# ScalarE's order within a step of a fused deformable convolution, attention and routing kernel

## The chip, the cores and the metric

The kernel runs on one core of one Trainium2 chip. The metric is device time in microseconds (us). The core has five engines with instruction streams of their own: TensorE (PE in the profile, its weight loads PEld), VectorE (DVE), ScalarE (ACT), GpSimd (POOL) and SyncE (SP), which only issues DMAs. An engine takes its stream in order; what belongs to another engine is waited for with semaphores.

## The reference, cut to what matters

The input holds 8 images of 128 channels and 56 x 56 pixels, in float32. The first layer adds a deformable convolution of the normalised image. The second treats the 3136 pixels of an image as tokens, adds causal attention, and then adds a mixture of 64 experts in which each expert takes its 8 best tokens of an image.

```
offset = conv3x3(groupnorm(x), offset_w) + offset_b        # 18 offsets for each pixel
x_off  = sum of 4 weighted gathers of groupnorm(x) at pixel + tap + offset   # 9 taps
x      = x + conv3x3_stride3(x_off, conv_w)

t      = tokens(x)                                          # (8, 3136, 128)
scores = (ln(t) Wq^T)(ln(t) Wk^T)^T / sqrt(128), causal
t      = t + softmax(scores) (ln(t) Wv^T)

probs  = softmax over the tokens of (ln(t) gate_w^T + gate_b)   # 64 experts
vals, idx = top 8 tokens of each expert
pooled = sum over the 8 of vals * token
out_e  = gelu([pooled, 1] weight1) weight2 (with bias row)
t      = t + scatter-add of out_e * vals to the tokens idx
```

## The kernel before

An image is 25 tiles of 128 pixels; 8 images make 200 tiles. One loop of steps runs over them, one step for a tile, and each engine has the same loop in its own stream. A step is a pipeline slice. In step s of image b:

- the convolution works on tile s of image b. Its nine gathered blocks of 128 x 128 are held in one of five ring buffers. ScalarE multiplies the first cell of each gathered pair by a weight (`scale_first`, L620, nine instructions in three pieces), VectorE adds the second (`add_second`, L889). Both work two or three tiles ahead of the tile that TensorE convolves. TensorE turns the nine blocks (`turn_samples`, L1201), ScalarE copies them out of PSUM (`keep_samples`, L625, three copies), and TensorE multiplies them (`products`, L1209);
- the scores are those of the tile six steps back (TensorE L1227, VectorE L901 adds the mask and takes the maximum, L1019 ends the maximum);
- softmax and attention are those of the tile seven steps back. ScalarE takes the exponentials (L721), TensorE turns the row of probabilities in pieces of 512 columns (`turn_prob`, L1236), ScalarE copies each piece to SBUF (`keep_prob`, L639), and TensorE multiplies it with the values (`attend`, L1250). VectorE adds the result to the tokens in the next step (L934, counted by `t2_done`), and only then may the next tile's attention overwrite the one PSUM bank of attention.

A tile i of an image has i + 1 blocks of 128 keys, so its row has one piece in tiles 0 to 3, two in tiles 4 to 7, three in tiles 8 to 11, and so on. Since attention runs seven steps behind, **one-piece steps are steps 7 to 10 of an image, and two-piece steps are 11 to 14**.

Everything else is hung into the steps by a table written by hand (MISC, L79 on). An entry says at which step, in which place of the step (E, F, M or L, in this order), which work for which image is done. TensorE fills a PSUM bank in that place (`fill_misc`) and ScalarE or VectorE empties it in the same place of its own stream (`keep_misc`). Those of place M in the steps concerned are the offset convolutions of the next image (`chunk`, steps 5 to 11, 12 matrix products of TensorE at L1111 and L1116, copied out by ScalarE at L648), the routing probabilities (`pm`, step 12), a block of queries (step 13) and the pooled tokens (step 14, emptied by VectorE). Place L holds `turn_xf` (L1141, copied at L665), `keys` (L1128, copied at L652), `query` (L1136, copied at L662) and `pm`.

All PSUM work but attention's sums goes through seven banks in a fixed order (RING_ORDER): a bank's seventh next user waits until its content was taken away.

The routing of the image before runs in steps 9 to 13: VectorE replaces the best eight logits (L1054, step 9), ScalarE takes exponentials of 64 x 3136 logits in four instructions (L737, two in step 10 and two in step 11), VectorE keeps the chosen ones (L1058). The next image's sampling indices are computed by VectorE in steps 13 to 17 (L830 to L862, nine instructions of it in step 13).

GpSimd issues nine indirect gathers for each tile, in order, as far ahead as the ring of five lets it. The last part of the kernel, from about 2576 us on, runs the experts and writes the output.

Of the kernel before, what the change touches and what calls it, by code (L numbers as in the profile page):

```python
# [11 lines left out]
ACT = mybir.ActivationFunctionType  # L12
# [3 lines left out]
B, C, H, W = 8, 128, 56, 56  # L16
# [77 lines left out]
LREPLACE, LEXP, LCHOSEN = 9, (10, 10, 11, 11), (11, 11, 12, 12)  # L94
SHARES = [(k, min(2 * CHUNK, N - k)) for k in range(0, N, 2 * CHUNK)]
# [10 lines left out]
def misc_at(step, place):  # L106

    b, s = divmod(step, TILES)
    return [(what, b + d, n) for t, at, what, d, n in MISC if t == s and at == place and 0 <= b + d < B]
# [45 lines left out]
def width_of(t):  # L155

    return (HALF_KEYS + 1 if split(t) else t % TILES + 1) * P


def chunks_of(i):  # L160

    total = width_of(i)
    return [(k, min(CHUNK, total - k)) for k in range(0, total, CHUNK)]


def chunks_in(t):

    return len(chunks_of(t % TILES)) if 0 <= t < ALL else 0
# [7 lines left out]
def rows_of(step):  # L176

    b, s = divmod(step, TILES)
    n = s - ROWS_STEP
    return [(b + 1, n)] if b + 1 < B and 0 <= n < ROW_GROUPS else []  # L180


def ahead(step):

    b, s = divmod(step, TILES)
    if b == 0 and s < AHEAD_TWO:
        return 1
    if AHEAD_THREE <= s < BACK_TO_TWO:
        return 3
    return 2  # L190
# [62 lines left out]
def image_of(t):  # L253

    return divmod(t, TILES)
# [72 lines left out]
def first_part(nc, x_cm, x_tok, off_w, off_b, conv_w, wq, wk, wv, gate_w, gate_b, w1, w2, base, b1_t, b2, pooled, ident, shared, w_in,  # L328
               c_base, c_ident, c_mask, c_group, pair_table, t2_dram, pm_dram, rz_dram):
    with ExitStack() as ctx:  # L330
        def sb(name, shape, dt=F32):
            return ctx.enter_context(nc.sbuf_tensor(name, shape, dt))
# [4 lines left out]
        def sem(name):  # L337
            return ctx.enter_context(nc.semaphore(name))
# [47 lines left out]
        logit = sb("logit", [E, NP])  # L386
        lmax = sb("lmax", [E, 1])
        zsum = sb("zsum", [E, len(SHARES)])
# [45 lines left out]
        replaced, lexp_done, rz_done, chosen = sem("replaced"), sem("lexp_done"), sem("rz_done"), sem("chosen")  # L434
# [11 lines left out]
        def prob_at(t, k0, w):  # L446

            start = 0 if t % 2 == 0 else PROB_COLS - width_of(t)
            return prob[:, start + k0:start + k0 + w]
# [149 lines left out]
        def _(act):  # L599
            after = Waits(act)  # L600

            def normalise(k, part):

                after(affine_done, k + 1)
                y0, y1 = part * H // PARTS, (part + 1) * H // PARTS
                inner = xpad[:].rearrange("p (y x) -> p y x", x=XW)[:, 1 + y0:1 + y1, 1:1 + W]
                given = first_image.rearrange("p (y x) -> p y x", x=W)[:, y0:y1, :] if k == 0 else inner
                act.activation(inner, given, ACT.Identity, bias=nb[:, 0:1], scale=rs[:, 0:1]).then_inc(normalised, 1)
# [14 lines left out]
            def keep_samples(t, p):  # L623
                after(smp_tp, PIECES * t + p + 1)
                act.activation(smp_t[p][:], ring_bank(("smp", t, p))[:, 0:3 * P], ACT.Copy).then_inc(smp_ev, 1)  # L625

            def keep_rows(k, n):

                at = ROW_GROUPS * k + n
                after(rows_tp, at + 1)  # L630
                after(rows_stored[at % 2], 32 * (at // 2))
                act.activation(rows_out[at % 2][:], ring_bank(("rows", k, n))[:].rearrange("p (i c) -> p i c", c=C),
                               ACT.Copy).then_inc(rows_ev, 1)

            def keep_prob(t, c):
                w = chunks_of(t % TILES)[c][1]
                q = CHUNKS_BEFORE[t] + c
                after(prob_tp, q + 1)
                act.activation(prob_t[q % 3][:, 0:w], ring_bank(("prob", t, c))[:, 0:w], ACT.Copy)\  # L639
                   .then_inc(prob_ev, 1)  # L640
# [37 lines left out]
            for h in range(2):  # L678
                at = h * HALF_IMAGE
# [28 lines left out]
            for step in range(END):  # L708
                b, s = image_of(step)
                v = step - LAG_V  # L710
                samples_first = step < ALL and chunks_in(step - LAG_S) == 1
                if samples_first:
                    for p in range(PIECES):
                        keep_samples(step, p)
                if 0 <= v < ALL:

                    r = v % 2
                    after(max_done, v + 1)
                    after(t2_done, v - 1)
                    row = prob_at(v, 0, width_of(v))  # L720
                    act.activation(row, row, ACT.Exp, bias=nmax[r][:, 0:1], accum_out=total[r][:, 0:1])\  # L721
                       .then_inc(exp_done, 1)
                if step < ALL and not samples_first:
                    for p in range(PIECES):
                        keep_samples(step, p)
                for use in misc_at(step, "E"):
                    keep_misc(use)
                for k, n in rows_of(step):
                    keep_rows(k, n)
                for use in misc_at(step, "F"):  # L730
                    keep_misc(use)
                if 0 <= b - 1 < B:
                    for k, (at, w) in enumerate(SHARES):
                        if s == LEXP[k]:
                            after(replaced, b)
                            after(rz_done, b - 1)
                            act.activation(logit[:, at:at + w], logit[:, at:at + w], ACT.Exp, bias=lmax[:, 0:1],  # L737
                                           accum_out=zsum[:, k:k + 1]).then_inc(lexp_done, 1)
                if chunks_in(v):
                    keep_prob(v, 0)  # L740
                parts = list(range(PARTS)) if s == NORMALISE and b + 1 < B else []
                early = chunks_in(v) >= 3
                pieces = sample_pieces(step)
                while pieces and not early:
                    scale_first(*pieces.pop(0))
                if chunks_in(v) >= 2:
                    keep_prob(v, 1)
                for c in inner_rounds(step):
                    if c + 1 < chunks_in(v):
                        keep_prob(v, c + 1)  # L750
                    if c == 1:
                        for use in misc_at(step, "M"):
                            keep_misc(use)
                    if early and pieces:
                        scale_first(*pieces.pop(0))
                    if c >= 2 and parts:
                        normalise(b + 1, parts.pop(0))
                for t, p in pieces:
                    scale_first(t, p)
                for use in misc_at(step, "L"):  # L760
                    keep_misc(use)
                for part in parts:
                    normalise(b + 1, part)
# [304 lines left out]
        def _(pe):  # L1068
            after = Waits(pe)
# [121 lines left out]
            for step in range(END):  # L1191
                ts, v = step - LAG_S, step - LAG_V
                b, i = image_of(step)
# [20 lines left out]
                def scores(c):  # L1214
                    tb, ti = image_of(ts)
                    k0, w = chunks_of(ti)[c]
                    emptied(after, ("query", tb, ti // PER))
                    free_ring(("score", ts, c))
                    k, at = GPI * tb + ti // PER, ti % PER * P
                    bank = ring_bank(("score", ts, c))  # L1220
                    if split(ts):
                        for h in range(2):
                            first = k0 + h * HALF_KEYS * P if k0 < HALF_KEYS * P else (TILES - 1) * P
                            last = pe.matmul(bank[h * ROWS_HALF:(h + 1) * ROWS_HALF, 0:w], qt[k % 2][:, at:at + ROWS_HALF],
                                             key_chunk(tb, first, w), start=True, stop=True)
                    else:
                        last = pe.matmul(bank[:, 0:w], qt[k % 2][:, at:at + P], key_chunk(tb, k0, w), start=True, stop=True)  # L1227
                    last.then_inc(scored, 1)
# [52 lines left out]
                for c in rounds:  # L1281
                    if c + 1 < chunks_in(v):
                        turn_prob(c + 1)
                    if c + 2 < chunks_in(ts):
                        scores(c + 2)
                    if c - 1 < chunks_in(v):
                        attend(c - 1)
                    if c == 1:
                        for use in misc_at(step, "M"):
                            fill_misc(use)  # L1290
                if rounds.stop - 1 < chunks_in(v):
# [337 lines left out]
```

## Time and profile before

| what | value |
|---|---|
| median of 3 runs | 2722.27 us (2721.83 to 2726.87) |
| the profiled execution | 2730.18 us |
| its span, first to last instruction | 2728.2 us |
| TensorE busy (PE) | 2547.9 us, 93% |
| weight loads busy (PEld) | 2044.1 us, 75% |
| VectorE busy | 1888.0 us, 69% |
| ScalarE busy | 1778.7 us, 65% |
| GpSimd busy | 1773.3 us, 65% |
| mean granted TensorE clock | 0.973 |

A busy share is that of the whole span; the ends of matrix products are modelled, and consecutive products overlap a little in the rows, so a distance between two starts tells more than a duration. The line numbers are those of the kernel file. Idle time of an engine stands in brackets behind the instruction that ended it, with what released it.

### The profile page before, as it was taken

How to read it: one execution, taken by the hardware profiler on the slowest of the kernel's cores; microseconds unless marked ns; L12 is line 12 of the kernel's file. 1: busy time of each engine (PE TensorE's matmuls, PEld its weight loads, DVE VectorE, ACT ScalarE, POOL GpSimd, SP SyncE). 2: the span in 40 equal slices, each digit the busy share in tenths (PEclk: the TensorE clock that was granted, in tenths of full speed). 3: DMA queues.
4: the chain of work that ended last, by engine and by line, in shares of the span. 5: the costliest groups of instructions: out<-in, count | busy, mean ns of one | idle time of the engine just before them, and what ended most of it. 6: DMA issues, size and time to landing. Idle time of an engine off the chain costs nothing. (4 is left out here: it accounts for less than half of the span.)

```text
span 2728.2 us, 53901 instructions
## 1 busy us (share of the span) xinstructions
PE 2547.9 (93%) x19262; PEld 2044.1 (75%) x19262; DVE 1888.0 (69%) x7300; ACT 1778.7 (65%) x4144; POOL 1773.3 (65%) x1831
## 2 busy tenths in 40 slices
PE   4688999999999999999999999999999998999687
PEld 3466787788878887788877887788778887787564
DVE  4456776886678767876688776877688766775425
ACT  3455667776677767677776767776777667765320
POOL 4777776777667775777677776777677776750000
PEclk8799999999999999999999999999999999999789
DMA  6354333653356334643356334634355333432299
GB/s 189 112 159 134 118 112 117 159 139 113 103 158 152 117 114 119 158 132 113 94 172 149 114 108 130 164 118 121 100 168 148 113 111 110 119 85 97 83 392 394
DMA packets 218149, 382.63 MB, mean 140 GB/s; under 512 B 43785, under 2 KB 128713, under 8 KB 216987
## 3 DMA queue, kind: packets, MB, share of 16 engines
q0 software_dynamic: 88992, 250.76, 31.6%
q1 hardware_dynamic: 126299, 113.98, 14.1%
q10 hardware_dynamic: 2592, 14.45, 1.3%
q8 instruction: 154, 2.52, 0.4%
q14 instruction: 112, 0.92, 0.1%
HBM read 316.92 MB, written 62.13 MB: 139 GB/s over the span
## 5 line engine op out<-in xcount | busy, mean ns | idle before, releaser
L592 POOL DMA_INDIRECT shared<-pair_table,idx x1800 | 1752.8, 974 | 670.8 <-issue 537.5
L1250 PEld LDWEIGHTS bank_o<-vals,prob_t 128*128 128x128 f32 x4800 | 583.9, 192 | 123.2 <-ACT prob_t L639 67.6
L1250 PE MATMUL bank_o<-vals,prob_t 128*128 128x128 f32 x4800 | 612.6, 277 | 38.3 <-ACT prob_t L639 38.3
L889 DVE SCALAR_TENSOR_TENSOR shared<-shared,wb 128x128 f32<-128x128 f32 x1800 | 514.5, 347 | 170.5 <-ACT shared L620 169.6
L639 ACT ACTIVATE prob_t<-bank_r 128x512 f32<-128x512 f32 (+2 forms) x704 | 369.8, 546 | 396.5 <-PE bank_r L1236 394.9
L620 ACT ACTIVATE shared<-shared,wa 128x128 f32<-128x128 f32 x1800 | 561.2, 391 | 65.8 <-DMA shared<-pair_table,idx 64.7
L901 DVE CUSTOM_DVE_ANT_0 prob<-bank_r,mask 128x512 f32<-128x512 f32 (+2 forms) x704 | 427.8, 624 | 239.1 <-PE bank_r L1227 220.3
L1227 PE MATMUL bank_r<-keys,qt 128*128 128x512 f32 (+3 forms) x1344 | 587.8, 554 | 0.8 <-ACT qt L662 0.3
L1209 PE MATMUL bank_r<-convw_t,smp_t 128*128 128x128 f32 x3600 | 479.5, 279 | 3.2 <-ACT smp_t L625 2.3
L1209 PEld LDWEIGHTS bank_r<-convw_t,smp_t 128*128 128x128 f32 x3600 | 443.3, 195 | 45.6 <-ACT smp_t L625 28.9
L1236 PE MATMUL bank_r<-ident,prob 128*128 128x128 f32 x2504 | 366.9, 273 | 4.1 <-ACT prob L721 4.0
L1227 PEld LDWEIGHTS bank_r<-keys,qt 128*128 128x128 f32 x1344 | 229.1, 194 | 143.3 <-issue 140.9
L721 ACT ACTIVATE prob<-prob,nmax 128x1664 f32<-128x1664 f32 (+23 forms) x200 | 325.2, 1626 | 14.8 <-DVE nmax L1019 13.5
L1236 PEld LDWEIGHTS bank_r<-ident,prob 128*128 128x128 f32 x2504 | 291.8, 141 | 19.2 <-issue 12.7
L1201 PE MATMUL bank_r<-ident,shared 128*128 128x128 f32 x1800 | 252.6, 285 | 54.2 <-DVE shared L889 54.2
L1201 PEld LDWEIGHTS bank_r<-ident,shared 128*128 128x128 f32 x1800 | 211.1, 146 | 77.7 <-DVE shared L889 67.7
L625 ACT ACTIVATE smp_t<-bank_r 128x384 f32<-128x384 f32 x600 | 249.4, 485 | 11.5 <-PE bank_r L1201 10.3
L1005 DVE TENSOR_TENSOR t<-bank_r,t 128x128 f32<-128x128 f32 x200 | 57.0, 285 | 133.9 <-PE bank_r L1209 133.9
L934 DVE SCALAR_TENSOR_TENSOR t<-bank_o,inv_total,t 128x128 f32<-128x128 f32 x192 | 67.3, 351 | 50.8 <-PE bank_o L1250 39.1
L1111 PE MATMUL bank_r<-shared,offw_t 128*32 128x448 f32 x896 | 97.9, 554 | 0.0
L1370 POOL MEMSET pooled_t<- 128x1024 f32 x1 | 1.0, 951 | 143.4 <-POOLq L330 143.4
L1132 PEld LDWEIGHTS bank_r<-wv_t,keys 128*128 128x128 f32 x400 | 54.6, 197 | 29.7 <-issue 29.7
(189 smaller groups left out, 2262.0 us busy)
## 6 DMA issues: line engine op xcount, KB each, us to landing
shared<-in_dram SPq DMA_DIRECT2D x32, 1024.0 KB, 18.0
shared<-pair_table,idx POOLq DMA_INDIRECT x1800
pair_table<-rows_out SPq DMA_DIRECT2D x112, 256.0 KB
t<-in_dram SPq DMA_DIRECT2D x48, 256.0 KB
t_dram<-t SPq DMA_DIRECT2D x48, 256.0 KB
shared<-in_dram SPq DMA_DIRECT2D x7, 1568.0 KB, 13.9
stage<-t_dram POOLq DMA_DIRECT2D x8, 832.0 KB, 7.4
pm_dram<-logit SPq DMA_DIRECT2D x8, 800.0 KB, 6.3
```

The costliest lines, as they stand in the source:

```text
L592: pool.indirect_dma_start(g[t % RING][:, n, :], None, pair_table[b % 2], bass.IndirectOffsetOnAxis(ap=idx[:, b % 2, i * TAPS + n:i * TAPS ...
L620: last = act.activation(first, first, ACT.Copy, scale=wa[:, b % 2, i * TAPS + n:i * TAPS + n + 1])
L625: act.activation(smp_t[p][:], ring_bank(("smp", t, p))[:, 0:3 * P], ACT.Copy).then_inc(smp_ev, 1)
L639: act.activation(prob_t[q % 3][:, 0:w], ring_bank(("prob", t, c))[:, 0:w], ACT.Copy)\
L721: act.activation(row, row, ACT.Exp, bias=nmax[r][:, 0:1], accum_out=total[r][:, 0:1])\
L889: last = dve.scalar_tensor_tensor(first, g[t % RING][:, n, C:], wb[:, b % 2, i * TAPS + n:i * TAPS + n + 1], first, ALU.mult, ALU.add)
L901: dve.tensor_tensor_reduce(prob_at(t, k0, w), ring_bank(("score", t, c))[:, 0:w], m, 1.0, NEG, ALU.add, ALU.max, cmax[t % 2][:, c:c + 1]). ...
L1201: last = pe.transpose(bank[:, n * P:(n + 1) * P], g[step % RING][:, 3 * p + n, 0:C], ident[:])
L1209: last = pe.matmul(ring_bank(("conv", step, 0))[:, 0:P], smp_t[p][:, n % 3 * P:(n % 3 + 1) * P], convw_t[:, n, :], start=(n == 0), stop=(n ...
L1227: last = pe.matmul(bank[:, 0:w], qt[k % 2][:, at:at + P], key_chunk(tb, k0, w), start=True, stop=True)
L1236: last = pe.transpose(ring_bank(use)[:, n * P:(n + 1) * P], prob_at(v, k0 + n * P, P), ident[:])
L1250: last = pe.matmul(attn_ps, prob_t[q % 3][:, n * P:(n + 1) * P], vals[:, slot(tb, at), :], start=(at == 0), stop=(at == ti))
```

## The change

Three edits, two in ScalarE's stream and one in TensorE's.

1. The routing's exponentials (L737) move behind the copies of the probabilities, the M work and the first scaled piece of the step; before, they stood ahead of the copy of the step's first probability piece.
2. The scaling of samples is "early" (one piece after each further copy of probabilities, the rest at the end of the step) also where the row has one or two pieces, if the step works two or more tiles ahead; before, it was so from three pieces on, and with one or two pieces all scaling came right after the first copy of probabilities. Steps ahead by two or more are all but the first 21 of image 0.
3. In one-piece steps TensorE fills the M work ahead of attention; before, behind its first piece. In all other steps the order stays.

```
             if chunks_in(v):
                 keep_prob(v, 0)
             parts = list(range(PARTS)) if s == NORMALISE and b + 1 < B else []
-            early = chunks_in(v) >= 3
+            early = chunks_in(v) >= 3 or ahead(step) >= 2
             pieces = sample_pieces(step)
             while pieces and not early:
                 scale_first(*pieces.pop(0))
...
                 if c >= 2 and parts:
                     normalise(b + 1, parts.pop(0))
+            if 0 <= b - 1 < B:
+                for k, (at, w) in enumerate(SHARES):
+                    if s == LEXP[k]:
+                        after(replaced, b)
+                        after(rz_done, b - 1)
+                        act.activation(logit[:, at:at + w], ... ACT.Exp ...).then_inc(lexp_done, 1)
             for t, p in pieces:
                 scale_first(t, p)
             for use in misc_at(step, "L"):
...
                 if c + 2 < chunks_in(ts):
                     scores(c + 2)
+                if c == 1 and chunks_in(v) == 1:
+                    for use in misc_at(step, "M"):
+                        fill_misc(use)
                 if c - 1 < chunks_in(v):
                     attend(c - 1)
-                if c == 1:
+                if c == 1 and chunks_in(v) != 1:
                     for use in misc_at(step, "M"):
                         fill_misc(use)
```

The block that the second hunk adds is removed, unchanged, from ahead of `keep_prob(v, 0)`.

## Rows read from the trace of the kernel before

**Rows 1.** Stretches of image 2: start:end, busy us (count) by engine, granted clock, DMA share.
```profile
769.68:848.09 78.41, 74.12 (x639) 59.08 (x638) 66.02 (x255) 56.46 (x152) 59.81 (x60) 1.00 0.62 161
848.09:963.91 115.82, 115.70 (x818) 95.21 (x818) 90.09 (x358) 84.44 (x196) 88.08 (x92) 1.00 0.46 130
1127.51:1130.92 3.41, 3.41 (x12) 2.64 (x12) 3.24 (x12) 2.81 (x7) 2.80 (x3) 0.50 0.28 77
```

**Rows 2.** Waits of the whole span: waiter, released by: total us, times, longest us.
```profile
ACT shared L620 <- DMA shared<-pair_table,idx: 64.7, 15, 12.1
POOL shared L592 <- PE bank_r L1201: 105.3, 35, 7.3
```

**Rows 3.** Timeline of TensorE, steps 7 to 14 of image 2 (start, us, line).
```profile
775.15 0.39 PE L1250 MATMUL bank_o<-vals,prob_t 128*128 128x128 f32 x2
...
777.01 0.38 PE L1116 MATMUL bank_r<-shared,offw_t 128*32 128x112 f32 x8
...
779.20 0.33 PE L1145 MATMUL bank_r<-xf_t,gate_t 128*64 128x64 f32 x2
...
785.62 0.66 PE L1128 MATMUL bank_r<-ident,vals 128*128 128x128 f32 x4 [0.92 <-DVE vals L982]
...
802.60 1.16 PE L1250 MATMUL bank_o<-vals,prob_t 128*128 128x128 f32 x8 [1.36 <-ACT prob_t L639]
...
814.32 0.37 PE L1116 MATMUL bank_r<-shared,offw_t 128*32 128x112 f32 x8
...
817.87 1.50 PE L1209 MATMUL bank_r<-convw_t,smp_t 128*128 128x128 f32 x12
...
823.82 0.71 PE L1250 MATMUL bank_o<-vals,prob_t 128*128 128x128 f32 x4 [1.09 <-ACT prob_t L639]
...
835.59 0.94 PE L1250 MATMUL bank_o<-vals,prob_t 128*128 128x128 f32 x6 [0.93 <-ACT prob_t L639]
...
839.64 1.50 PE L1209 MATMUL bank_r<-convw_t,smp_t 128*128 128x128 f32 x12
...
842.52 1.06 PE L1250 MATMUL bank_o<-vals,prob_t 128*128 128x128 f32 x8
```

**Rows 4.** Timeline of ScalarE, the same steps.
```profile
774.99 2.74 ACT L620 ACTIVATE shared<-shared,wa 128x128 f32<-128x128 f32 x9
777.63 0.52 ACT L648 ACTIVATE offs<-bank_r 128x448 f32<-128x448 f32 x1
778.05 0.26 ACT L665 ACTIVATE xf_t<-bank_r 128x128 f32<-128x128 f32 x1
...
801.97 0.57 ACT L639 ACTIVATE prob_t<-bank_r 128x512 f32<-128x512 f32 x1
...
808.99 1.14 ACT L737 ACTIVATE logit<-logit,lmax 64x1024 f32<-64x1024 f32 x1
...
810.12 0.34 ACT L737 ACTIVATE logit<-logit,lmax 64x64 f32<-64x64 f32 x1
...
815.20 0.93 ACT L721 ACTIVATE prob<-prob,nmax 128x768 f32<-128x768 f32 x1
...
816.12 1.24 ACT L625 ACTIVATE smp_t<-bank_r 128x384 f32<-128x384 f32 x3
...
836.89 1.15 ACT L721 ACTIVATE prob<-prob,nmax 128x1024 f32<-128x1024 f32 x1
```

**Rows 5.** Timeline of VectorE, the same steps.
```profile
813.10 2.44 DVE L889 SCALAR_TENSOR_TENSOR shared<-shared,wb 128x128 f32<-128x128 f32 x9
815.46 2.34 DVE L1058 SCALAR_TENSOR_TENSOR logit<-prob,logit 64x1024 f32<-64x1024 f32 x2
...
836.00 0.62 DVE L830 TENSOR_TENSOR pos<-pos,off_bias 128x450 f32<-128x450 f32 x1
...
841.23 0.35 DVE L934 SCALAR_TENSOR_TENSOR t<-bank_o,inv_total,t 128x128 f32<-128x128 f32 x1
```

**Rows 6.** Timeline of TensorE, step 10 of image 7.
```profile
2311.16 1.40 PE L1250 MATMUL bank_o<-vals,prob_t 128*128 128x128 f32 x8 [3.23 <-ACT prob_t L639]
```

More of the change, by code:

```diff
@@ L731, in _ @@
                     keep_misc(use)
[L732 to L738, printed above, removed]
                 if chunks_in(v):
@@ L741, in _ @@
                 parts = list(range(PARTS)) if s == NORMALISE and b + 1 < B else []
-                early = chunks_in(v) >= 3
+                early = chunks_in(v) >= 3 or ahead(step) >= 2
                 pieces = sample_pieces(step)
@@ L757, in _ @@
                         normalise(b + 1, parts.pop(0))
+                if 0 <= b - 1 < B:
+                    for k, (at, w) in enumerate(SHARES):
+                        if s == LEXP[k]:
+                            after(replaced, b)
+                            after(rz_done, b - 1)
+                            act.activation(logit[:, at:at + w], logit[:, at:at + w], ACT.Exp, bias=lmax[:, 0:1],
+                                           accum_out=zsum[:, k:k + 1]).then_inc(lexp_done, 1)
                 for t, p in pieces:
@@ L1285, in _ @@
                         scores(c + 2)
+                    if c == 1 and chunks_in(v) == 1:
+                        for use in misc_at(step, "M"):
+                            fill_misc(use)
                     if c - 1 < chunks_in(v):
                         attend(c - 1)
-                    if c == 1:
+                    if c == 1 and chunks_in(v) != 1:
                         for use in misc_at(step, "M"):
```

## The prediction

> **What bounds the kernel now.** I read the stretches by engine first, then the waits, then the timelines of three engines over one image. Images 1 to 6 repeat each other, so image 2 stands for them. In steps 15 to 24 TensorE is busy for 115.70 of 115.82 us; in steps 7 to 14, the ones changed, for 74.12 of 78.41 [rows 1]. So TensorE's own stream sets the time, and these eight steps hold 4.3 us of gaps: 0.92 behind VectorE's values (step 8), and 1.36, 1.09 and 0.93 behind a copy of probabilities (steps 10, 12, 13) [rows 3]. Gathers don't bind: ScalarE waited for them 15 times in all [rows 2], for over 0.4 us only in the prologue, in image 0 and in step 19 of image 7, and GpSimd waits for free ring buffers instead (105.3 us).
>
> **What goes.** Edits 1 and 2 put `keep_prob` ahead of the logit exponentials and of nine scalings. The three gaps behind probabilities go: 1.36 + 1.09 + 0.93 = 3.38 us an image. Edit 3 moves a chunk's products (about 1.9 us) ahead of attention; TensorE's work stays the same, and VectorE takes attention's sums only in the next step.
>
> **What comes.** In ScalarE's loop the copy of the M work now stands ahead of the scaling, and it can't start before TensorE has filled it. Before, ScalarE scaled during that fill: nine scalings took 774.99 to 777.63, and the chunk's copy followed as TensorE finished it at 777.39 [rows 3, 4]. Now the scaling, 2.64 us, starts behind that copy, and all that ScalarE does next for TensorE comes that much later. For each step I add ScalarE's path from the end of the M products to the copy that TensorE needs next, and TensorE's from there to its use. A handover costs 0.06 (copy ended at 802.54, TensorE started at 802.60 [rows 3, 4]); there are two in each path.
>
> - Step 7 to 8: ScalarE 0.12 + chunk copy 0.42 + scalings 2.64 + `xf_t` copy 0.26 = 3.44 [rows 4]. TensorE: 777.39 to 779.20 is 1.81, and 0.32 for the attention that now comes behind the chunk: 2.13 [rows 3]. New gap 1.31. VectorE gets its samples later too, so the gap before `keys` stays at some 0.69 instead of 0.92.
> - Steps 8 to 9 and 9 to 10, added the same way (the copies awaited are `keys` and `qt`, of 128x512 like the 0.57 in [rows 4]): 0.24 and 1.05.
> - Step 10 to 11: no scaling, but the two long exponentials (2 x 1.14 [rows 4]) now stand between the chunk's copy and the next softmax: 0.30.
> - Step 11 to 12, the dearest. TensorE needs 814.69 to 817.87 = 3.18 from the chunk's end to the next convolution products [rows 3]. ScalarE needs 0.12, chunk copy 0.43, three scalings 0.88, exponentials 1.46, six scalings 1.76, softmax 0.92 (815.20 to 816.12) and the first of three sample copies, about 0.45 of 1.24 [rows 4]: 6.0. New gap 2.83.
> - Step 12, VectorE. Its last samples of step 11 are ready 4.7 us behind the chunk's end. With 0.88 for the last three additions they end 5.6 behind it; before, 815.54 - 814.69 = 0.85 [rows 3, 5]. It is 4.75 later, TensorE 2.83; the logits' selection (2.34 [rows 5]) follows and nothing absorbs the difference. The score bank that the second piece needs comes 0.63 late, and `keys` waits 1.12 for values.
> - Step 13 to 14: ScalarE 0.12 + `qt` 0.5 + scalings 2.64 + `pm` 0.12 + softmax 1.13 + sample copy 0.45 = 4.96 [rows 4]. TensorE from attention's second piece to the products: 835.59 to 839.64, less 0.1 of overlap, 3.95 [rows 3]. New gap 1.0.
> - Step 14, VectorE: after its late samples it has nine index instructions (836.00 to 841.03) and the sum of attention, ended at 841.58; TensorE's attention started at 842.52, 0.94 to spare [rows 3, 5]. With VectorE about 7.3 later than before and TensorE 4.5, this becomes a gap of 1.95.
>
> Added: 1.31 + 0.69 + 0.24 + 1.05 + 0.30 + 2.83 + 0.63 + 1.12 + 1.0 + 1.95 = 11.1. Gone: 0.92 + 3.38 = 4.3, and about 0.4 more, because a gap in the rows starts at the modelled end, some 0.1 behind the point where the next group could have started. Net +6.4 us an image. From step 15 on all engines are late by the same, and TensorE has no idle time to give it back.
>
> There are six such images: 6 x 6.4 = 38.5 us. Image 0 has only edit 3, in steps where TensorE waits for gathered samples anyway: nothing. Image 7 has no chunk; its gap of 3.23 in step 10 [rows 6] goes, the losses of steps 11 to 14 come, and its gathers are just in time at step 19 (one of the waits of [rows 2]), so I take 0, between -3 and +3.
>
> The clock: after the gap of step 12 in image 3 the granted clock was 0.50, the lower level of 1.2 GHz, over 1127.51 to 1130.92 [rows 1], which costs 1.7 us of work where nothing hides it; image 4 has one more like it, the other four none. The new gaps are longer. What the clock adds where the trace has no such gap is between 0 and 1.7 us an image; half of it may be hidden behind the new waits. I take +2 us over all, net of the two that were there.
>
> Sum: 38.5 + 2 = +40.5 on the profiled execution's 2730.18 (span 2728.2 and 2.0 around it), which is 7.9 above the median of the runs. The difference goes onto the median: 2722.3 + 40.5 = 2763 us.
>
> **Rivals.**
> - *Faster: ScalarE's new waits stay free.* The point that decides is step 12's first convolution product: if ScalarE's path there were under TensorE's 3.18, only gains were left, 6 x 3.38 = 20, and up to 3 in image 7: 2699. For it: ScalarE is busy for only 56.46 of 78.41 us [rows 1], and the M work is short. Against it: its idle time lies ahead of the M copy, where it can't be used in order. 7%.
> - *ScalarE late, VectorE not.* The gaps that I got through VectorE (0.63 + 1.12 + 1.95 = 3.7 an image) don't come if its late samples slide into idle time that I overlooked: +2.7 an image, 16 in all, 2738. For it: VectorE idles 12.4 us in these steps [rows 1]. Against it: most of that is ahead of step 12. 17%.
> - *The lower clock in each image.* One unhidden slice of 1.7 an image on top: 38.5 + 10 = 2771; with further waits that grow behind it, 2780. For it: every gap before was shorter than 2.83 in these images, and the clock fell twice. Against it: in the steps that follow, TensorE waits for VectorE anyway. 15%.
> - *TensorE catches up.* 2722, the losses hidden later. Steps 15 to 24 speak against it: 0.12 us of idle time in 115.82 [rows 1], and TensorE's products there keep the same distances whatever came before. 4%. The Trainium skill (Perfetto Trace Analysis, Identifying the Most-Contended Engine) says that busy time of matrix products is no good measure of how near TensorE is to its limit, and asks for the busy share of weight loads; that share is 95.21 of 115.82, 82% [rows 1]. By that rule 18% of the stretch, 20 us, would be room to absorb 6.4; by the row with the gaps there is none, and I go by the gaps.
>
> **How the numbers follow.** My forecast has 57%. All but the first and the last rival are slower: 57 + 17 + 15 = 89% slower by over 0.2%, which is 5.4 us and about what a measurement of this kernel can tell from no change; 4% within it; 7% faster. The range reaches from just under the second rival to the end of the third: 2736 to 2780. It leaves out the faster case, the one that catches up, and the tails.
>
> **What would show it.** In the profile after, steps 8 to 15: the gaps of TensorE behind `prob_t` are gone in images 1 to 6; in their place one of nearly 3 us ahead of the products of step 12, released by ScalarE's sample copies, and one ahead of attention in step 14, released by VectorE's L934. ScalarE waits for L1116 ahead of its scalings, and VectorE waits longer for L620. Steps 7 to 14 take 78.4 + 6.4 = 84.8 us an image, steps 15 to 24 the same 115.8. I am wrong if ScalarE's scaling starts before the chunk's products end, if the gap of step 12 is under 1 us, or if steps 15 to 24 change.

## The result and the profile after

The changed kernel takes 2770.61 us, the median of four runs (2766.95 to 2774.71); the kernel before, run beside it, 2724.57 (four runs, 2721.83 to 2728.43). The ratio is 1.0168, with a 95% interval of 1.0153 to 1.0184: slower by 46.0 us. Forecast were 2763 us and +40.5, with a range of 2736 to 2780.

First the page of the changed kernel: its span and busy times, and TensorE's clock over 40 slices.

```profile
span 2765.0 us, 53901 instructions
PE 2561.4 (93%) x19262; PEld 2052.3 (74%) x19262; DVE 1890.2 (68%) x7300; ACT 1774.7 (64%) x4144; POOL 1756.9 (64%) x1831
PEclk8789999999999999999999999999999999999799
```

The shares are within one per cent of the span of those of before; the page alone tells nothing of the cause. The stretches of image 2 tell where the time is: steps 7 to 14, steps 15 to 24, and one slice at the lower clock, a stretch with a granted clock of 0.50, which is 1.2 GHz (columns as in [rows 1]).

```profile
771.85:858.08 86.23, 77.23 (x639) 60.97 (x638) 66.98 (x255) 55.99 (x152) 65.48 (x67) 0.98 0.61 158
858.08:973.89 115.81, 115.69 (x818) 95.21 (x818) 90.06 (x358) 84.38 (x196) 87.79 (x93) 1.00 0.47 130
825.47:828.88 3.41, 3.41 (x18) 3.41 (x17) 3.28 (x12) 0.51 (x2) 2.94 (x2) 0.50 0.57 152
```

Steps 7 to 14 took 78.41 us and take 86.23, 7.82 more; steps 15 to 24 took 115.82 and take 115.81 [rows 1]. All of the loss of image 2 is in the eight steps that the change touches, and nothing is given back behind them.

TensorE in these steps (start, us, line, and in brackets the idle time before with what ended it):

```profile
779.26 0.49 PE L1250 MATMUL bank_o<-vals,prob_t 128*128 128x128 f32 x2
782.92 0.33 PE L1145 MATMUL bank_r<-xf_t,gate_t 128*64 128x64 f32 x2 [1.43 <-ACT xf_t L665]
789.04 0.66 PE L1128 MATMUL bank_r<-ident,vals 128*128 128x128 f32 x4 [0.50 <-DVE vals L982]
801.99 1.35 PE L1227 MATMUL bank_r<-keys,qt 128*128 128x512 f32 x4 [1.06 <-ACT qt L662]
807.99 1.16 PE L1250 MATMUL bank_o<-vals,prob_t 128*128 128x128 f32 x8
812.27 1.60 PE L1209 MATMUL bank_r<-convw_t,smp_t 128*128 128x128 f32 x12 [0.41 <-ACT smp_t L625]
824.81 2.37 PE L1209 MATMUL bank_r<-convw_t,smp_t 128*128 128x128 f32 x12 [2.70 <-ACT smp_t L625]
831.29 0.71 PE L1250 MATMUL bank_o<-vals,prob_t 128*128 128x128 f32 x4
842.45 0.83 PE L1250 MATMUL bank_o<-vals,prob_t 128*128 128x128 f32 x6
847.54 1.60 PE L1209 MATMUL bank_r<-convw_t,smp_t 128*128 128x128 f32 x12 [0.98 <-ACT smp_t L625]
852.44 1.13 PE L1250 MATMUL bank_o<-vals,prob_t 128*128 128x128 f32 x8 [1.75 <-DVE t L934]
```

The attentions at 807.99, 831.29 and 842.45 have lost their brackets: the waits for `prob_t` of [rows 3] are gone, as the edits say. Five others of 0.98 to 2.70 us and a short one (0.41) stand elsewhere; the gap ahead of the keys of step 8 is still there and falls from 0.92 to 0.50. In image 5 there is one more, ahead of the keys of step 12 (image 3 has it too, 1.68):

```profile
1762.82 0.63 PE L1128 MATMUL bank_r<-ident,vals 128*128 128x128 f32 x4 [1.69 <-DVE vals L982]
```

ScalarE of the changed kernel in steps 7, 11 and 13 shows what they wait for.

```profile
779.40 0.54 ACT L648 ACTIVATE offs<-bank_r 128x448 f32<-128x448 f32 x1 [2.27 <-PE bank_r L1116]
779.97 2.74 ACT L620 ACTIVATE shared<-shared,wa 128x128 f32<-128x128 f32 x9
782.61 0.25 ACT L665 ACTIVATE xf_t<-bank_r 128x128 f32<-128x128 f32 x1
...
818.83 0.55 ACT L648 ACTIVATE offs<-bank_r 128x448 f32<-128x448 f32 x1 [2.66 <-PE bank_r L1116]
819.27 0.98 ACT L620 ACTIVATE shared<-shared,wa 128x128 f32<-128x128 f32 x3
820.15 1.14 ACT L756 ACTIVATE logit<-logit,lmax 64x1024 f32<-64x1024 f32 x1
...
821.61 1.85 ACT L620 ACTIVATE shared<-shared,wa 128x128 f32<-128x128 f32 x6
823.36 0.93 ACT L721 ACTIVATE prob<-prob,nmax 128x768 f32<-128x768 f32 x1
...
842.65 0.60 ACT L662 ACTIVATE qt<-bank_r 128x512 f32<-128x512 f32 x1 [1.26 <-PE bank_r L1136]
843.14 2.73 ACT L620 ACTIVATE shared<-shared,wa 128x128 f32<-128x128 f32 x9
```

Read the bracket of L648 together with the line below it. ScalarE stood idle for 2.66 us until TensorE had filled the chunk, and only then began nine scalings that needed nothing of that chunk. Before, the nine ran inside that idle time: in step 7 from 774.99, and the chunk's copy followed at 777.63 [rows 4].

VectorE of the changed kernel in steps 11 and 13:

```profile
820.28 0.88 DVE L889 SCALAR_TENSOR_TENSOR shared<-shared,wb 128x128 f32<-128x128 f32 x3 [3.62 <-ACT shared L620]
822.62 1.75 DVE L889 SCALAR_TENSOR_TENSOR shared<-shared,wb 128x128 f32<-128x128 f32 x6 [1.46 <-ACT shared L620]
824.29 2.35 DVE L1058 SCALAR_TENSOR_TENSOR logit<-prob,logit 64x1024 f32<-64x1024 f32 x2
...
844.15 2.63 DVE L889 SCALAR_TENSOR_TENSOR shared<-shared,wb 128x128 f32<-128x128 f32 x9 [2.71 <-ACT shared L620]
846.70 0.62 DVE L830 TENSOR_TENSOR pos<-pos,off_bias 128x450 f32<-128x450 f32 x1
...
851.32 0.39 DVE L842 TENSOR_SCALAR prob<-pos 128x225 f32<-128x225 f32 x1
851.74 0.16 DVE L964 RECIPROCAL inv_total<-total 128x1 f32<-128x1 f32 x1
851.94 0.35 DVE L934 SCALAR_TENSOR_TENSOR t<-bank_o,inv_total,t 128x128 f32<-128x128 f32 x1
```

It waits 3.62, 1.46 and 2.71 us for the late scalings. Behind the last wait it works for 7.8 us without a pause before it comes to attention's sum at 851.94, and TensorE's attention, which waits for that sum, starts at 852.44.

### The profile page after: what moved, and what is told of

It reads as the page before. It is cut to its first block and busy times, and to the rows that moved or that the text cites. A ratio compares the mean times of both kernels' runs of the same rounds, so it can differ in the third digit from the quotient of the medians.

```text
span 2765.0 us, 53901 instructions
## 1 busy us (share of the span) xinstructions
PE 2561.4 (93%) x19262; PEld 2052.3 (74%) x19262; DVE 1890.2 (68%) x7300; ACT 1774.7 (64%) x4144; POOL 1756.9 (64%) x1831
## 5 line engine op out<-in xcount | busy, mean ns | idle before, releaser
L1209 PE MATMUL bank_r<-convw_t,smp_t 128*128 128x128 f32 x3600 | 487.7, 282 | 30.0 <-ACT smp_t L625 29.1
L648 ACT ACTIVATE offs<-bank_r 128x448 f32<-128x448 f32 x56 | 30.3, 541 | 104.8 <-PE bank_r L1116 104.7
L934 DVE SCALAR_TENSOR_TENSOR t<-bank_o,inv_total,t 128x128 f32<-128x128 f32 x192 | 67.3, 351 | 43.1 <-PE bank_o L1250 31.5
```

The lines of the kernel that those rows point to most:

```text
L1209: last = pe.matmul(ring_bank(("conv", step, 0))[:, 0:P], smp_t[p][:, n % 3 * P:(n % 3 + 1) * P], convw_t[:, n, :], start=(n == 0), stop=(n ...
```

## The experiments

The theory: edit 2 alone makes the loss, because it puts ScalarE's copy of the M work, which waits for TensorE, ahead of scalings that wait for nothing; what is late then passes through ScalarE and VectorE to TensorE. The rivals were that edit 1 (the exponentials) or edit 3 (the fill ahead of attention) costs it, and, later, that the gaps of step 14 are carried over from step 12. The table gives each run's median and its ratio to the kernel before on the same chip. "7 to 14" is what these steps of image 2 take more than before, from the first `turn_samples` of step 7 to that of step 15 in the two profiles; the last column is the mean over the six whole images 1 to 6.

| kernel | median us | ratio (95%) | 7 to 14 | per image |
|---|---|---|---|---|
| the changed kernel | 2770.61 | 1.0168 (1.0153 to 1.0184) | +7.8 | +8.0 |
| without edit 2 | 2719.25 | 0.9986 (0.9975 to 0.9996) | -0.8 | -1.4 |
| edit 2 alone | 2806.29 | 1.0316 (1.0298 to 1.0333) | +11.6 | +12.4 |
| edit 3 alone | 2714.19 | 0.9960 (0.9947 to 0.9973) | -1.7 | -2.3 |
| edit 1 alone | 2728.10 | 1.0014 (1.0003 to 1.0025) | +0.5 | 0.0 |
| without edit 1 | 2774.31 | 1.0173 (1.0151 to 1.0195) | +8.2 | +8.5 |
| scaling ahead of the M copy, step 11 | 2749.23 | 1.0094 (1.0075 to 1.0112) | +5.4 | +3.3 |
| the same, step 13 | 2762.87 | 1.0130 (1.0112 to 1.0149) | +5.8 | +6.1 |
| the same, all short steps | 2714.65 | 0.9971 (0.9960 to 0.9983) | -1.8 | -2.4 |
| that, exponentials split | 2710.35 | 0.9949 (0.9937 to 0.9961) | -2.4 | -3.0 |
| index work split | 2771.86 | 1.0168 (1.0153 to 1.0184) | +7.1 | +8.1 |
| both of the last two | 2711.71 | 0.9950 (0.9937 to 0.9963) | -3.9 | -2.7 |
| that, keys later | 2714.60 | 0.9956 (0.9943 to 0.9970) | -3.8 | -2.6 |

The slices at the lower clock are in both columns. The profile before has two, in step 13 of its images 3 and 4 (12.78 and 12.81 us where the other images take 11.12); a kernel without them thus looks 0.6 us better in the last column.

### Which edit

**Without edit 2**, from the changed kernel:

```
-            early = chunks_in(v) >= 3 or ahead(step) >= 2
+            early = chunks_in(v) >= 3
```

> Edits 1 and 3 without edit 2: in one- and two-piece steps the nine scalings stand right behind the first copy of probabilities again, ahead of the M copy. Theory (ScalarE's M copy ahead of the scalings is what costs): the new gaps ahead of L1145 (1.43), L1227 (1.06) and the products of step 12 (2.70) go. The gap of 1.36 in step 10 goes, about 0.4 comes in step 11, about 0.2 in step 12; 1.09 and 0.93 in steps 12 and 13 stay. Some -0.9 us in each of images 1 to 6 and up to -3 in image 7: about 2716 us where before is 2724.6, ratio 0.997 (0.995 to 0.999). Rival A (the logit exponentials' new place costs most): the gap ahead of step 12's products stays over 2 us, 2745 or more, ratio over 1.007. Rival B (attention behind the chunk delays VectorE): the step after each one-piece step stays longer by 0.5 or more, ratio 1.004 or more.

Measured 0.9986, inside what was expected. All five gaps of more than 0.9 us are gone, and the two behind `prob_t` that edit 2 removes are back; TensorE at the 0.31 that is left in step 11, and at the first of the two:

```profile
804.57 1.60 PE L1209 MATMUL bank_r<-convw_t,smp_t 128*128 128x128 f32 x12 [0.31 <-ACT smp_t L625]
820.56 0.71 PE L1250 MATMUL bank_o<-vals,prob_t 128*128 128x128 f32 x4 [1.10 <-ACT prob_t L639]
```

So neither edit 1 nor edit 3 makes the loss; both rivals fall.

**Edit 2 alone**, the reverse one-line edit made to the kernel before.

> The kernel before with edit 2 alone: only the scalings are moved behind the further copies and the M copy. Theory: nearly the whole loss is in this edit. Gaps ahead of L1145 1.7, keys 0.5, L1227 1.3, products of step 12 about 1.3 (the exponentials' 1.46 now lies elsewhere), step 14 1.0 and 1.75; the 1.36 of step 10 stays, 1.09 and 0.93 go. About +6 us an image, 2760 us, ratio 1.013 (1.009 to 1.016). Rival A (exponentials): at most +10 us over all, ratio under 1.004. Rival B (attention's place): as before, ratio 1.000 to 1.004.

Measured 1.0316, more than twice the loss expected. The largest part of the surplus is in step 10, which takes 5.0 us more in image 2; a wait of 0.59 for the copied keys in step 9 (0.9 us longer) and one of 1.57 for VectorE's values in step 12 (2.1 us longer) were not expected either. TensorE, then ScalarE, then VectorE in step 10:

```profile
816.41 1.36 PE L1250 MATMUL bank_o<-vals,prob_t 128*128 128x128 f32 x8 [2.78 <-ACT prob_t L639]
```

```profile
813.51 1.15 ACT L737 ACTIVATE logit<-logit,lmax 64x1024 f32<-64x1024 f32 x1 [1.69 <-DVE prob L1054]
...
815.78 0.57 ACT L639 ACTIVATE prob_t<-bank_r 128x512 f32<-128x512 f32 x1
```

```profile
807.15 2.63 DVE L889 SCALAR_TENSOR_TENSOR shared<-shared,wb 128x128 f32<-128x128 f32 x9 [3.31 <-ACT shared L620]
...
810.07 3.40 DVE L1054 MATCH_REPLACE8 prob<-top,logit 64x3136 f32<-64x3136 f32 x1
```

The late scalings make VectorE's additions late (wait 3.31), with them the replacement of logits (L1054), on which the exponentials wait 1.69 us; and without edit 1 the copy of the probabilities still stands behind these. The chain runs through two engines and back, and the expectation had not followed it. With edit 3 beside it the same gap is 0.94 (below), with edits 1 and 3 none. In image 2 a lower clock comes on top: over 817.00 to 820.40 the granted clock was 0.53. Image 1 has no such slice; there step 10 is 3.5 us and the whole image 10.1 us longer.

**Edit 3 alone** and **edit 1 alone**, each made to the kernel before as the change has it.

> The kernel before with edit 3 alone: TensorE fills the chunk ahead of attention in one-piece steps, ScalarE's order is that of before. Theory: in step 10 the chunk's 1.9 us hide the copy of probabilities behind the exponentials, so the gap of 1.36 goes (-1.5 in step 10) and nothing comes, since the scalings still run during the fill: -1.6 us in each of images 1 to 6, nothing in image 7: 2713 us where before is 2723, ratio 0.9965 (0.995 to 0.998). Rival (attention behind the chunk delays VectorE and costs): ratio 1.000 or more, with steps 8 to 11 longer.

Measured 0.9960, as expected: the gap of 1.36 ahead of attention in step 10 goes, step 10 is 1.51 shorter, steps 11 to 24 are the same within 0.06 us. Edit 3 by itself is a gain.

> The kernel before with edit 1 alone: only the logit exponentials are moved. Theory: the gap of 1.36 in step 10 goes, but the two exponentials now stand behind the chunk's copy and delay the next softmax: a gap of some 1.3 ahead of step 11's products, and 0.35 more in step 12, so +0.3 us in each of images 1 to 6 and about -1 in image 7: 2725 us where before is 2724, ratio 1.000 (0.998 to 1.002). Rival A (the exponentials' place costs by itself): ratio 1.004 or more.

Measured 1.0014, about nothing. Step 10 is 1.34 shorter and step 11 1.53 longer: the exponentials, moved behind the chunk's copy, hold up the sample copies of the next step.

```profile
806.30 1.60 PE L1209 MATMUL bank_r<-convw_t,smp_t 128*128 128x128 f32 x12 [1.25 <-ACT smp_t L625]
```

**Without edit 1**, edits 2 and 3 only.

> Edits 2 and 3 without edit 1: the logit exponentials stand ahead of the first copy of probabilities. In e2 this place made step 10 4 us longer, because VectorE's replaced logits, for which the exponentials wait, came late with the late samples. Theory: with the chunk ahead of attention 1.9 us of that are hidden, a gap of some 1.2 stays in step 10 (step 10 about +1.5 more than in the changed kernel); steps 11 and 12 are shorter by 0.5 and 1.5. About -0.5 us an image against the changed kernel: 2766 us, ratio to before 1.0155 (1.011 to 1.020). Rival A (the exponentials behind the M copy cost most): 2745 or less, ratio under 1.008.

Measured 1.0173 against 1.0168 with it: no difference. The gap of step 12 falls from 2.70 to 1.24, by the 1.46 that the exponentials took among its late scalings (820.15 to 821.61); but a gap of 0.94 behind `prob_t` opens in step 10, and step 13 of image 2 is 1.0 us dearer, because the slice at the lower clock (0.50 over 839.07 to 842.48) now lies mostly in it (from 839.86 on) and not under a wait.

The price of edit 2 thus depends on the company: +3.2% alone, 1.73 + 0.40 = 2.1% beside edit 3, 1.68 + 0.14 = 1.8% beside both. Parts measured one at a time don't add up here.

### The order as the cause

**Scalings ahead of the M copy.** The probabilities still go first, but the scalings stand ahead of the copy that waits. From the changed kernel, in ScalarE's loop over pieces:

```
                 if c + 1 < chunks_in(v):
                     keep_prob(v, c + 1)
+                if c == 1 and chunks_in(v) < 3:
+                    while early and pieces:
+                        scale_first(*pieces.pop(0))
                 if c == 1:
                     for use in misc_at(step, "M"):
                         keep_misc(use)
```

> The changed kernel with one swap: in steps of one or two pieces all scalings stand behind the copies of probabilities, but ahead of the M copy. Theory: every new gap goes and the old ones behind probabilities stay away: steps 7 to 9 as before, step 10 -1.1, step 12 -1.0, step 13 -0.9, some -3.3 us in each of images 1 to 6 and -2 to -3 in image 7: 2702 us, ratio 0.992 (0.989 to 0.995). Rival A: the exponentials stand behind the M copy as in the changed kernel, so step 12's gap stays over 2 us and the time over that of before, ratio over 1.000. Rival B: steps 8 to 11 stay longer than before by 0.5 each, ratio near 1.000.

Measured 0.9971 against 1.0168: this order alone is worth 2%, which is what the theory says. ScalarE in step 11 of image 2 now scales between the probabilities and the chunk's copy, which then doesn't wait:

```profile
806.73 2.73 ACT L620 ACTIVATE shared<-shared,wa 128x128 f32<-128x128 f32 x9
809.51 0.55 ACT L648 ACTIVATE offs<-bank_r 128x448 f32<-128x448 f32 x1
```

But 0.992 was expected. Steps 10, 12 and 13 gain 1.51, 0.82 and 1.19 us; step 14 loses 1.37 through a gap that the kernel before doesn't have:

```profile
836.56 1.13 PE L1253 MATMUL bank_o<-vals,prob_t 128*128 128x128 f32 x8 [0.94 <-DVE t L937]
```

(L937 is L934 of before.) VectorE still waits 0.84 us for the scalings in step 13 and has its nine index instructions ahead of the sum. TensorE has become the earlier of the two.

**In step 11 only, in step 13 only**: the same with `s == 11` or `s == 13` in place of `chunks_in(v) < 3`.

> The changed kernel, but in step 11 alone the scalings stand ahead of the M copy. Theory: step 12's gap ahead of the products falls from 2.70 to some 0.3 and VectorE is no longer late there, so step 12 gives back some 4 us; steps 8 to 10 and the gaps of step 14 (0.98 and 1.75, which form anew in step 13) stay. Some -4 us in each of images 1 to 6: 2746 us, ratio to before 1.0085 (1.006 to 1.011). Rival (VectorE's lateness of step 14 is carried on from step 11): the gap ahead of attention in step 14 goes too, 2735 or less, ratio under 1.0045.

> The changed kernel, but in step 13 alone the scalings stand ahead of the M copy (the queries'). Theory: step 14's gap ahead of the products (0.98) goes and the one ahead of attention (1.75) falls to 0.4 to 0.9, since VectorE gets its samples of step 13 some 2.6 us earlier; steps 8 to 12 stay. Step 14 goes from +3.2 to some +0.7, about -2.5 us in each of images 1 to 6: 2755 us, ratio to before 1.0115 (1.009 to 1.0145). Rival (VectorE's lateness of step 14 comes from step 11): the 1.75 stays or grows, ratio 1.015 or more.

Measured 1.0094 and 1.0130. With step 11 mended, step 12 goes from 3.56 us over before to 0.83 under it, worth 1.0168 - 1.0094 of 2724 us, some 20 us, nearly half of the loss. (In step 14 image 2 has a slice at the lower clock, as 1.88 for eight products shows, so its +5.4 stands above the mean.) The gaps of step 14 stay, so they are made in step 13 and not carried over:

```profile
843.30 1.60 PE L1212 MATMUL bank_r<-convw_t,smp_t 128*128 128x128 f32 x12 [0.98 <-ACT smp_t L625]
848.40 1.88 PE L1253 MATMUL bank_o<-vals,prob_t 128*128 128x128 f32 x8 [1.95 <-DVE t L937]
```

With step 13 mended, the first of these goes and the second shrinks from 1.75 to 1.10, where 0.4 to 0.9 was expected; it is still L937 of VectorE that ends it. Both ratios lie inside what was expected.

**Exponentials split.** On top of the order above, the two long ones (step 10) stand right behind the first copy of probabilities and the two of step 11 ahead of it. `routing_exps(step)` issues the exponentials of that step; its definition and the removal of edit 1's block are left out here:

```
+            routing_exps(LEXP[-1])      # those of step 11
             if chunks_in(v):
                 keep_prob(v, 0)
+            routing_exps(LEXP[0])       # those of step 10
```

> As e3, but the two exponentials of step 11 stand ahead of the first copy of probabilities as before (ScalarE was idle there), and the two of step 10 right behind that copy, ahead of the M copy. Theory: the 0.4 in step 11 and 0.2 in step 12 go too: some -3.6 us an image, 2699 us, ratio 0.991 (0.988 to 0.993), the fastest of the four. Rival A: the two exponentials of step 11 matter more than the swap, so this is 10 us or more faster than e3. Rival B: the same as e3 within 1 us.

Measured 0.9949, the lowest of all and by the ratios 2.2% faster than the changed kernel; the loss of step 11 (0.53) goes too. It beats both kernels. But 0.991 was expected: the gap behind VectorE in step 14 stays (1.10), and the step is 1.52 us longer than before. From edit 3 alone (0.9960) its interval doesn't tell it apart.

### The limit behind it

**Index work split.** Of the five parts of the sampling indices, two stand in step 13; here the second of them goes to step 14, and the part of step 14 to step 15.

```
-INDEX = (13, 13, 14, 16, 17)
+INDEX = (13, 14, 15, 16, 17)
```

> The changed kernel with VectorE's index work of step 13 split: the second half (four instructions, 2.4 us) in step 14, what was in step 14 in step 15. Theory: the gap of 1.75 ahead of attention in step 14, released by VectorE's L934, goes, the one ahead of the products (0.98) stays: -1.75 in each of images 1 to 6, 2759 us, ratio to before 1.013 (1.011 to 1.0155), 10 us under the changed kernel. Rival (VectorE is late by the samples alone): the gap of 1.75 stays within 0.3, 2769 us, or the same time comes back as a gap in steps 15 or 16.

> As e4 (scalings ahead of the M copy, exponentials split), with VectorE's index work spread over steps 13, 14 and 15. In e4 step 14 was 1.5 us longer than before, with a gap of 1.10 ahead of attention released by VectorE's L934: there VectorE's stream, not ScalarE's, ate the gain of steps 12 and 13. Theory: that gap goes, -1.1 to -1.5 in each of images 1 to 6: 2702 us, ratio 0.992 (0.990 to 0.994), and images 1 to 6 take 297.8 us each in place of 299.4. Rival (VectorE stays behind in any order): the gap moves to step 15 or 16 and the time is that of e4, 0.995.

Made to the changed kernel, and to the fastest. Measured 1.0168 and 0.9950, where 1.013 and 0.992 were expected; as the rivals say, the gap moves. The one of step 14 behind L934 goes in both, and one of 1.51 comes in step 16. (In the first run the slice at the lower clock lies in step 13 of images 1 to 5, 0.50 over 838.75 to 842.16 in image 2, so the table's 7.1 understates what steps 7 to 14 gained. In image 6, where it lies under the wait of step 12, steps 7 to 14 are 5.9 longer than before, against 7.7 in the changed kernel, and step 16 is 1.7 longer.) TensorE of the first, steps 12, 14 and 16:

```profile
836.93 0.63 PE L1128 MATMUL bank_r<-ident,vals 128*128 128x128 f32 x4 [1.56 <-DVE vals L982]
...
853.87 1.60 PE L1209 MATMUL bank_r<-convw_t,smp_t 128*128 128x128 f32 x12 [0.98 <-ACT smp_t L625]
...
882.92 0.63 PE L1128 MATMUL bank_r<-ident,vals 128*128 128x128 f32 x4 [1.51 <-DVE vals L982]
```

**Keys later**: on top of that, the keys that wait there move from the end of step 16 into step 17.

```
-    (16, "E", "logit", 0, 1), (16, "L", "keys", 0, 3),
-    (17, "E", "vals", 0, 3), (17, "M", "query", 0, 3),
+    (16, "E", "logit", 0, 1),
+    (17, "E", "keys", 0, 3), (17, "F", "vals", 0, 3), (17, "M", "query", 0, 3),
```

> As e8, and the keys that TensorE turned at the end of step 16 are turned in step 17 (place E, their values in place F). In e8 the only gap that was new against before was one of 1.51 there, behind VectorE's normalised tokens. Theory: VectorE is behind by a fixed amount, not for good, so the gap goes and none comes in step 17: -1.6 us in each of images 1 to 6, 2703 us, ratio 0.9915 (0.990 to 0.9935). Rival (VectorE's stream is full from step 12 to 17 and the gap moves on): the time of e8, 0.995.

Measured 0.9956, the time of the run before, as the rival says. Step 16 loses its gap and, without the keys, is 0.44 us shorter than before; step 17, with them, takes 2.13 us more, and TensorE waits behind VectorE there in two places. The two steps together take 1.69 us more than before, where they took 1.70 more without this edit. (The line numbers of this kernel and of the next rows stand 6 above those of before.)

```profile
861.98 2.84 PE L1233 MATMUL bank_r<-keys,qt 128*128 128x512 f32 x6 [0.39 <-DVE t L1011]
...
869.25 1.16 PE L1242 MATMUL bank_r<-ident,prob 128*128 128x128 f32 x7 [0.65 <-DVE cmax L907]
```

Twice the gap moved to the next place where TensorE needs VectorE, and the time stayed. VectorE's own waits say why. In the run with both, image 2, these two waits stand next to each other:

```profile
840.65 0.23 DVE L927 COPY pooled<-bank_r 128x64 f32<-128x64 f32 x1 [1.18 <-PE bank_r L1166]
...
872.51 2.63 DVE L895 SCALAR_TENSOR_TENSOR shared<-shared,wb 128x128 f32<-128x128 f32 x9 [2.24 <-ACT shared L620]
```

From 840.65 to 870.27, where the second wait begins, that is in steps 15 to 17, it waits for nothing. In that stretch moving its work gained nothing; taking work away from it there wasn't tried, so that this would help is not shown.

## Why the prediction was right

The mechanism, its places and the sign were right. Its terms against the gaps in the profile after, image 2 where no other is named:

| step of the prediction | expected | profile after |
|---|---|---|
| gaps behind `prob_t` | gone | gone |
| step 8, behind `xf_t` | 1.31 | 1.43 |
| step 8, ahead of keys | 0.69 | 0.50 |
| steps 9 and 10 | 0.24, 1.05 | step 9 0.23 longer; 1.06 |
| step 11 | 0.30 | 0.41 |
| step 12, behind `smp_t` | 2.83 | 2.70 |
| step 12, through VectorE | 0.63 + 1.12 = 1.75 | 1.68, 1.69 (images 3, 5), all ahead of the keys |
| step 14, behind `smp_t` | 1.0 | 0.98 |
| step 14, behind L934 | 1.95 | 1.75 (1.95, 1.90 in images 3, 5) |
| steps 15 to 24 | no change | -0.01 |

By the prediction's own terms the gap behind L934 comes to 7.3 - 4.5 - 0.94 = 1.86 and not 1.95, which changes nothing here.

**The mis-sized term** is the step from gaps to time, "about 0.4 more, because a gap in the rows starts at the modelled end". By their brackets the gaps of after come to 1.43 + 0.50 + 0.23 + 1.06 + 0.41 + 2.70 + 1.68 + 0.98 + 1.75 = 10.7, against 11.1 expected and 4.3 before. That is +6.4, my net figure, but steps 7 to 14 are 7.8 longer. Most gaps cost more than their bracket, those that come no less than those that go, and I had granted it only to those that go. The runs show the size: edit 3 alone takes away a bracket of 1.36 and step 10 is 1.51 shorter; in the run with the index work split 1.51 comes in step 16 and the step is 1.71 longer; a gap of 0.94 makes step 14 1.37 longer with the scalings ahead. That is 0.1 to 0.4 us a gap, and there are about twice as many gaps as before. It doesn't hold for each: with edit 1 alone the same 1.36 goes and step 10 is only 1.34 shorter. Why the surplus differs stays open.

**The clock.** I took 2 us net. After the gap of 2.70 the granted clock was 0.50 in image 2 over 825.47 to 828.88, from 0.7 us after TensorE began again. Such a slice now stands in each of images 1 to 6, in image 1 twice. In image 2 it costs next to nothing, because TensorE would have waited for VectorE ahead of the keys anyway: their bracket of 1.69 in image 5 is missing there, and step 12 takes 14.15 us there and 14.27 in image 5. In images 3 and 5 it comes behind that wait, and the second one of image 1 is in step 14. Set against image 2 of the kernel before, these three images are 9.4 us longer and the other three 7.7 to 7.8, so an unhidden slice costs some 1.6 us. The run with step 13 alone mended, whose step 12 has the same gap of 2.70, bears this out: its image 5 has no slice at all and is 5.9 us longer, image 2 with the slice under the wait 5.8, images 3 and 6 with the slice behind it 7.5. Three slices, less the two of before at some 1.7 each ([rows 1] shows one), make +1.4.

**The sum.** Images 1 to 6 are 9.4, 7.8, 7.7, 6.1, 9.4 and 7.7 longer, 48.1 in all with the clock, against 38.5 + 2. Image 7 is 2.7 shorter, inside my bounds of -3 and +3. That makes 45.4; the medians differ by 46.0. That the two agree so closely is partly luck: in the twelve experiments image 7 took between 1.5 us less and 2.8 more than in the profile before. The forecast was helped by it too: its term for the gaps was some 8 us too low (six images at 7.8 less the 38.5), and image 7, put at nothing, hid 2.7 of them. Of the 7.6 us between 2763 and 2770.6, 2.3 are in the kernel before, whose median I put at 2722.3 and which took 2724.6 beside the change. The two profiled executions differ by only 2766.95 - 2730.18 = 36.8, because image 0 and what is ahead of it took 7.3 us less in the one after and the tail 1.4 less. In the twelve experiments the stretch up to the end of image 0 was only 0.5 to 2.9 shorter than in the profile before. In that stretch lie nearly all of ScalarE's waits for gathers, and it differs by up to 7.3 us from profile to profile, so the difference belonged on the median.

**The rivals.** That ScalarE's waits stay free falls with the gap of 2.70; that VectorE isn't late falls with 1.75 in step 14 and 1.69 in step 12. That the lower clock comes in each image was half right: it comes, but four of the seven slices lie under another wait, which leaves +1.4 us in all and not 10. That TensorE catches up falls in every run: steps 15 to 24 of image 2 take the same within 0.05 us, except where work was moved into them. The Trainium skill (Perfetto Trace Analysis, Identifying the Most-Contended Engine) judges TensorE's headroom by the share of peak arithmetic and by the busy share of weight loads; by the second, an estimate of 18% of room. The rows disagree: weight loads are busy for 95.21 of 115.81 us, and nothing is caught up.

## What to carry to other kernels

On an engine that works in order, an instruction that must wait for another engine belongs behind the work that waits for nothing; here, moving copies ahead because their reader waits was a gain only where the copy that waits did not move ahead with them. Follow what becomes late through every engine to the one that sets the time, and expect a new gap to cost some tenths of a microsecond more than its bracket, as most did here. When a gap only moves and the time stays, look whether the engine behind it ever waits; if not, moving its work gains nothing.

## What the runs showed of the hardware

Two things I had not expected. A gap in TensorE's rows mostly cost 0.1 to 0.4 us more than its bracket (1.36 and 1.51, 1.51 and 1.71, 0.94 and 1.37; but also 1.36 and 1.34). And the granted clock fell to 0.50 in each of six images behind a gap of 2.70 us or the one that followed it. Where that slice lay under a wait for VectorE it cost nothing that the length of the steps shows (5.8 us for image 2 of the run with step 13 mended, 5.9 for its image 5, which has none), and behind it it cost some 1.6 us.
